# A local-attention stack on one core: squares summed as rows, norms spread by one-hot matmuls, q scaled right behind k, two passes reordered

## The reference

```python
q, k, v = split(x @ Wqkv)                      # 16 heads of width 64
q = l2norm(q) * q_scale;  k = l2norm(k) * k_scale
q = q*cos*scale + rotate_half(q)*sin*scale     # k with 1/scale
out = local_attention(q, k, v)                 # windows of 32, each looks at itself and the one before
x = x + out @ Wo
x = x + (a * gelu(gate)) @ W2                  # a, gate = split(layernorm(x) @ W1 + b1)
```

## Time and profile before

| | before |
|---|---|
| median of 3 runs | 4742.06 us (4739.58 to 4746.09) |
| the profiled execution, its own time | 4749.81 us |
| its span in the profile | 4748.0 us |
| busy PE / DVE / ACT / POOL | 93% / 74% / 52% / 52% |
| pass a0, first slots to the stack | about 0 to 580 us |
| stack (48 bodies) | about 580 to 4060 us |
| rotated pass and gated mix | about 4060 to 4748 us |

### The profile page before, as it was taken

One profiled execution on the slowest core, in us unless ns is written; L12 is line 12 of the kernel. 1 busy time (PEld: TensorE's weight loads), 2 busy tenths in 40 slices (PEclk: granted clock), 3 DMA queues, 4 the chain that ended last, 5 costly groups with the idle time before them and its releaser, 6 DMA issues. The chain is left out here.

```text
span 4748.0 us, 116556 instructions
## 1 busy us (share of the span) xinstructions
PE 4426.3 (93%) x46020; PEld 2614.7 (55%) x46020; DVE 3530.1 (74%) x3768; ACT 2451.6 (52%) x3764; POOL 2477.3 (52%) x3513
## 2 busy tenths in 40 slices
PE   7999889999999999999999999999999998678898
PEld 3333366666666666666666666666666665322233
DVE  5777478777778778778778778778778776477774
ACT  1666545554555555555455555545555554135564
POOL 1111266666666666666566666666666665122213
PEclk6999989999999999999999999999999999779999
DMA  3222122222222222222222223222222222222220
GB/s 88 56 55 55 55 51 63 57 58 71 63 61 61 55 74 72 53 61 61 73 65 59 57 60 81 57 62 57 57 72 58 58 61 71 42 55 46 48 45 19
DMA packets 182135, 281.98 MB, mean 59 GB/s; under 512 B 58269, under 2 KB 80349, under 8 KB 175965
## 3 DMA queue, kind: packets, MB, share of 16 engines
q1 hardware_dynamic: 154300, 241.72, 21.4%
q10 hardware_dynamic: 27648, 37.79, 3.5%
HBM read 61.77 MB, written 17.56 MB: 17 GB/s over the span
## 5 line engine op out<-in xcount | busy, mean ns | idle before, releaser
L1144 DVE SCALAR_TENSOR_TENSOR x<-l_r,l_qkvec,l_tab 128x1024 f32<-128x1024 f32 x768 | 936.3, 1278 | 31.0 <-ACT l_sq L1047 27.9
L553 DVE TENSOR_REDUCE a_nmax<-a_pair 128x2 f32<-128x1024 f32 x512 | 609.4, 1220 | 223.4 <-PE a_pair L676 223.3
L453 ACT ACTIVATE a_pt<-a_st 128x512 f32<-128x512 f32 x1024 | 543.2, 603 | 281.6 <-PE a_st L660 276.3
L974 POOL TENSOR_TENSOR l_ntmp<-l_seed 128x32 f32<-128x32 f32 (+1 forms) x480 | 112.1, 234 | 777.9 <-ACT l_seed L1030 759.1
L1001 POOL TENSOR_TENSOR l_u<-x 128x512 f32<-128x512 f32 x384 | 491.4, 1280 | 0.0
L1002 POOL TENSOR_TENSOR l_u<-x 128x512 f32<-128x512 f32 x384 | 490.2, 1276 | 0.0
L1317 PE MATMUL l_r<-xs,l_wqkv 128*128 (+1 forms) x768 | 424.6, 660 | 38.8 <-DVEq L1224 38.8
L1406 PE MATMUL l_r<-l_pbd,l_va 128*64 128x160 f32 (+1 forms) x6144 | 441.2, 296 | 18.8 <-DMA l_pbd<-l_pt 18.7
L1007 POOL TENSOR_TENSOR l_p<-l_p,l_srec 128x1024 f32<-128x1024 f32 x192 | 365.4, 1903 | 175.3 <-DVE l_srec L1236 142.0
L1406 PEld LDWEIGHTS l_r<-l_pbd,l_va 128*64 128x64 f32 x6144 | 395.3, 137 | 80.1 <-issue 80.0
L1367 PE MATMUL l_r<-l_kbd,l_qn 64*32 64x128 f32 x24576 | 418.5, 279 | 12.2 <-DMA l_kbd<-l_kn 6.6
(11 more groups left out here) (204 smaller groups left out, 7452.7 us busy)
## 6 DMA issues: line engine op xcount, KB each, us to landing
l_kbd<-l_kn SPq DMA_DIRECT2D x1536, 64.0 KB, 2.0
l_pbd<-l_pt SPq DMA_DIRECT2D x768, 64.0 KB
l_pbd<-l_pt ACTq DMA_DIRECT2D x576, 64.0 KB
a_ks<-a_scr SPq DMA_DIRECT2D x96, 192.0 KB
a_qs<-a_scr SPq DMA_DIRECT2D x288, 64.0 KB
a_scr<-a_parts SPq DMA_DIRECT2D x48, 256.0 KB, 2.5
l_pbd<-l_pt SPq DMA_DIRECT2D x192, 56.0 KB
l_wqkv<-in_wqkv SPq DMA_DIRECT2D x6, 1536.0 KB, 6.5
```

Source lines behind the costliest of these rows:

```text
L453: nc.scalar.activation(pt[n % 2][:, r, :], st[(4 * n + r + par) % 3][:], ACT.Exp, scale=SC).then_inc(exp_done, 1)
L553: nc.vector.tensor_reduce(out=nmax[:, n, 2 * i:2 * i + 2], in_=pair[i][:], op=ALU.max, axis=AX.X, negate=True).then_inc(pair_dve[i], 1)
L1144: last = nc.vector.scalar_tensor_tensor(out=t[a][:, 2 * half:2 * half + 2, :], in0=R[a][:, half, :].unsqueeze(1).to_broadcast([D, 2, T]), ...
```

## The change

In the stack:

- The squares of k are no longer added on POOL: TensorE adds the halves itself. The sums are made with the new matrix `block8` (8 columns) as the stationary side and the squares as the moving side, four groups of 128 tokens in four column tiles of the array, so that a head's sums stand as a row of 128 tokens. The norms become a 128x128 tile instead of 128x32, and so do the seed, the Newton steps, the reading on DVE and the zeros that clear R[3].
- ACT's expansion and the eight transposes go; `spread8`, a one-hot matrix of 64 rows to 128 columns, spreads the rows with eight matmuls, with a wait of PE for itself between the fourth and the fifth.
- q is scaled right behind k, ahead of the row sum.
- In the first three steps DVE turns P between the rotations of q and k. In the fourth step the sums of squares move up to the start, q is rotated before the residual is added, and v is projected between the mean and the variance.

In the rotated pass `QK_STEP` goes from 4 to 2, `ROWS_STEP` from 8 to 10, the splits from slots 6, 7, 7, 8, 9 to 5, 6, 7, 8, 9, and SP reads the row maxima behind the heads as in pass a0.

```diff
-        QK_STEP, ROWS_STEP = (4, 9) if rope is None else (4, 8)
+        QK_STEP, ROWS_STEP = (4, 9) if rope is None else (2, 10)
...
-                if m is not None and rope is not None:
-                    load_rows(0, par)
                 if s is not None:
...
-                if m is not None and rope is None:
+                if m is not None:
                     load_rows(0, par)
...
-                split_slots = (4, 5, 6, 7, 8) if rope is None else (6, 7, 7, 8, 9)
+                split_slots = (4, 5, 6, 7, 8) if rope is None else (5, 6, 7, 8, 9)
...
-        NSS = NT * 2 * CH
-        rnx = sb("rnx", [D, NSS, HALF])
+        NSS = D
+        spread8 = sb("spread8", [D, 2, 2, D])
...
-                        nc.gpsimd.tensor_tensor(sqs[0][:], sq[0][:, 0, :], sq[0][:, 1, :], ALU.add)
-                        nc.gpsimd.tensor_tensor(sqs[1][:], sq[1][:, 0, :], sq[1][:, 1, :], ALU.add).then_inc(S["sq_sum"], 1)
+                        nc.gpsimd.tensor_tensor(sqs[:], sq[0][:, 0, :], sq[0][:, 1, :], ALU.add).then_inc(S["sq_sum"], 1)
...
 ACT
-                    if has_ss and c < 3:
+                    if has_ss:
                         seeds(0, NSS, S["norm_ready"], S["seed_ready"])
...
+                        act.drain().then_inc(S["sq_ready"], 1)
...
-                        act.drain().then_inc(S["sq_ready"], 1)
+                        act.drain().then_inc(S["sqk_ready"], 1)
...
-                    if has_ss and c == 3:
-                        seeds(0, NSS, S["norm_ready"], S["seed_ready"])
...
-                    if has_ss:
-                        expand()
...
 DVE
-                    transpose_p(c)
+                    if c == 3 or b is None:
+                        transpose_p(c)
+                    if has_ss and c == 3:
+                        read_norm()
+                    if c == 3 and b is not None:
+                        rotate(0)
...
+                        nc.vector.engine_nop().then_inc(S["centred_pe"], 1)
...
-                    if c == 3 and has_ss:
-                        read_norm()
...
                     if b is not None:
-                        rotate(0)
+                        if c < 3:
+                            rotate(0)
+                            transpose_p(c)
                         rotate(1)
...
                         scale_by_norm(1)
-                        if c == 3:
-                            scale_by_norm(0)
+                        scale_by_norm(0)
...
-                    if has_ss and c < 3:
-                        scale_by_norm(0)
...
 PE
                         claim(3)
+                        pe.wait_ge(S["sqk_ready"], seen.next(S["sqk_ready"]))
+                        for half in range(2):
+                            for k in range(NT):
+                                nc.tensor.matmul(R[3][32 * k:32 * k + 2 * CH, 0, 0:D], block8[:, 1, :], sq[1][:, half, 128 * k:128 * k + 128],
+                                                 start=False, stop=False, skip_group_check=True)
                         pe.wait_ge(S["sq_sum"], seen.next(S["sq_sum"]))
                         for k in range(NT):
-                            for a in range(2):
-                                o = (k * 2 + a) * CH
-                                last = nc.tensor.matmul(R[3][:, 0, o:o + CH], sqs[a][:, 128 * k:128 * k + 128], block4[:],
-                                                        start=False, stop=True, skip_group_check=True)
+                            last = nc.tensor.matmul(R[3][32 * k:32 * k + 2 * CH, 0, 0:D], block8[:, 0, :], sqs[:, 128 * k:128 * k + 128],
+                                                    start=False, stop=True, skip_group_check=True)
...
-                    if has_ss and c < 3:
+                    if has_ss:
                         sums_of_squares()
...
-                    if c == 3 and has_ss:
-                        sums_of_squares()
...
+                    if has_var:
+                        pe.wait_ge(S["centred_pe"], seen.next(S["centred_pe"]))
+                    if b is not None:
+                        project_v()
+                    if has_var:
...
-                        pe.wait_ge(S["rnx_ready"], seen.next(S["rnx_ready"]))
+                        pe.wait_ge(S["rn_ready"], seen.next(S["rn_ready"]))
                         claim(0, "r0_dve_b", "r0_dve_b")
-                        for a in (1, 0):
-                            for k in range(NT):
-                                o = (k * 2 + a) * CH
-                                last = nc.tensor.transpose(R[0][:, 1 - a, 128 * k:128 * k + 128],
-                                                           rnx[:, o:o + CH, :].rearrange("p h i -> p (h i)"), C["ident"][:])
+                        for turn in range(2):
+                            for k in range(2):
+                                for half in range(2):
+                                    rows, a, o = slice(64 * half, 64 * half + 64), (half + turn + 1) % 2, 256 * half + 128 * k
+                                    last = nc.tensor.matmul(R[0][:, 1 - a, o:o + 128], spread8[rows, a, k, :], rn[rows, 0:D], start=True, stop=True)
+                                    if turn == 0:
+                                        last.then_inc(S["b_turn"], 1)
+                            if turn == 0:
+                                pe.wait_ge(S["b_turn"], seen.next(S["b_turn"], 4))
```

57 lines of the change are left out of this document (29 added, 28 removed).

## The result

| | before | after |
|---|---|---|
| median | 4743.43 us (4739.58 to 4746.09, 4 runs) | 4972.14 us (4960.14 to 4985.12, 4 runs) |
| ratio, 95% interval | 1 | 1.0483 [1.0455, 1.0512] |
| span of the profiled execution | 4748.0 us | 4983.3 us |

The change makes the kernel 4.8% slower: +229 us, where the forecast had +46 and its range ended at 4855 us. The direction was right, the size was not.

A forecast was written before the change was run, and what follows sets the result against it. It took DVE to bound a body's first steps and a chain through PE and DVE the rest; stack +89, clock -19, rotated pass -26, constant +2 gave +46 us, 4788 us against the median, range 4725 to 4855 us.

The forecast's parts named there:

- H: DVE, from reading the norms to rotating q: wait for q's square, now uncovered, plus wider norms; 1.29 us.
- the fifth boundary: PE, five tiling-mode changes a step instead of four: at most 19 us by the rows, possibly a whole drain each.
- The fourth step's chain: Stack's fourth step, third step's maximum until the scores begin: 21.19 us, with PE standing still for reading, seed and mask.
- the extra constant: Start of the stack: the additional constant adds some 2 us.
- a quarter back: Stack: low clock costs 74 us; sums go but new standstills come, so a quarter is regained, -19 us.
- the second loop: First steps: P's copies, product with v, new sums, q's projection and square, two rotations, P again; 13.1 us.
- DVE's at the 13.43 of the forecast: First steps, bounded by DVE: 13.43 us against 13.32, the removed POOL wait replaced by one as long.
- PE's wait for itself: Spread of the norms on PE: between nothing and 0.6 us, taken as 0.2.
- a clean body: One body of the stack without low clock: 1.89 us longer, 71.7 us; +89 us over 47 bodies.
- The clock was one: Rival, chance 0.18, faster: denser records keep the clock high in stack and rotated pass, giving 4707 us.
- The other three: Rivals: in between (0.10, no change, 4733 to 4750); tiles don't overlap (0.05, 5070); POOL becomes the bound (0.05, 4940).
- the tiles that don't overlap: Rival, chance 0.05, slower: sums on PE take 3.05 us, +8 us a body, 5070 us.

The follow-up runs named there:

- the new arithmetic alone: Changed kernel with DVE and ACT orders as before; sums as rows, k's halves on PE, spread by matmuls and the rotated pass's edits stay: 4824.13 us, ratio 1.0156.
- products in all three gaps: Changed kernel plus one unused product ahead of P by V in the first two steps, two ahead of the fourth step's scores: 4850.58 us, ratio 1.0208.
- The two fastest kernels: Rotated pass's edits; fourth step sums, last Wo products, q, mean, k; norms read behind P's turn: 4703.73 us (new sums and spread), 4703.26 us (old).

## Why the prediction was wrong in size

**What held.** Slower. H: in DVE's timeline of one body of after, 1.25 us lie between reading the norms and rotating q, where the forecast had 1.29:

```profile
1350.24 0.23 DVE L1166 TENSOR_SCALAR l_norm<-l_r 128x128 f32<-128x128 f32 x1
1351.49 2.48 DVE L1133 SCALAR_TENSOR_TENSOR x<-l_r,l_qkvec,l_tab 128x1024 f32<-128x1024 f32 x2 [1.02 <-ACT l_sq L1045]
```

POOL isn't the bound: its 128-column operations take 0.40, 0.46, 0.30 and 0.46 us, and the new arithmetic alone leaves the first two steps at 13.3 and 13.5. The sums overlap in their column tiles: 24 records from 1366.18 to the next start at 1366.95, 0.77 us, the forecast's 0.8, and this holds the change of tile shape to the projection behind them, so the fifth boundary has no cost that shows:

```profile
1366.18 0.62 PE L1296 MATMUL l_r<-l_sq,l_block 128*8 128x128 f32 x16
1366.95 1.98 PE L1313 MATMUL l_r<-xs,l_wqkv 128*128 x4
```

The fourth step's chain came out nearly term by term. In the body whose scores were shown above it takes 21.68 us from the third step's maximum (1283.39) to the scores (1305.07), against 21.19. The residual to the centring takes 1299.93 - 1297.15 = 2.78 us (forecast 2.79), PE waits 1.59 us for the mask; only H is longer there, 1294.75 - 1292.96 = 1.79 us instead of 1.29, because q's projection comes late on PE:

```profile
1292.96 0.29 DVE L1166 TENSOR_SCALAR l_norm<-l_r 128x128 f32<-128x128 f32 x1
1294.75 2.48 DVE L1133 SCALAR_TENSOR_TENSOR x<-l_r,l_qkvec,l_tab 128x1024 f32<-128x1024 f32 x2 [1.50 <-ACT l_sq L1045]
1297.15 0.68 DVE L1179 TENSOR_TENSOR xs<-xs,l_r 64x512 f32 x1
...
1299.93 0.69 DVE L1184 TENSOR_TENSOR l_xcn<-xs,l_r 128x512 f32<-128x512 f32 x1 [1.38 <-PE l_r L1330]
```

The rotated pass gives 19 us where the forecast had 26. The 2 us for the extra constant were not tested.

**The clock had the wrong sign.** The forecast took -19 us, "a quarter back", since the sums went. It named the new standstills in the same place and gave them no price. What it was can be read from the bodies whose mean granted clock is 1.00. In before they are 14 of 46, with a median of 69.80 us; in the changed kernel with products in all three gaps 35 of 46, with a median of 72.66. The mean bodies are 71.43 and, of after, 76.74, so the low level cost 1.6 us a body in before and costs 4.1 in after. This term was about +115 instead of -19: 134 of the missing 183 us. The experiment agrees: in that run the changed kernel needs 122 us less, though part of this is low clock that before has too. The term has two places. In the first two steps the products with v ran at the low level in many bodies, means of 3.0 and 2.8 us instead of 2.29; in the fourth the scores had a mean of 3.04 us instead of 2.36 (the spans of these groups, each step by itself). For the first two steps "it is idle time of an engine that no longer bounds this step" is the sentence that failed: the wait was free, what it did to the speed of the next product was not, and that product is in the loop. In the fourth step the forecast had the wait in its chain and the scores behind it at their old length, 24.22 us less the terms it named; that was wrong in the same way.

The Trainium skill's page "TensorE: Matmul & The Clock Gate", Part 4, has transposes not counted as PE activity as matmuls are; by it the change should have helped the clock. The two fastest kernels have the same order, one with transposes and one with matmuls (and with the old and the new sums), and mean clocks of 0.961 and 0.968 at the same time: the rule's sign may be right, but nothing came of it here.

**A loop without slack.** The forecast had the second loop at 13.1 us. The same sum by the rows of the run with P turned between the rotations, with the new sums, is 4.21 + 2.10 + 2.22 + 0.77 + 1.91 + 2.40 = 13.6 (in after itself the medians of the first two are 4.19 and 2.09); the term that was mis-sized is the way to the fifth copy, 4.21 + 2.10 instead of 3.81 + 2.0. So it was this loop, not DVE's at the 13.43 of the forecast, that bound, and the second step's median is 13.59. A loop that is itself the bound has nothing that could take up a slow product: every one at the low level went straight into the step.

**The third step is PE's.** I read it as part of one chain of DVE from the third maximum to the next body's, because the averages of the earlier trace rows don't separate steps. The step of before has no PE idle at all, and that of after, in windows, nearly none:

```profile
1605.90:1623.40 17.50, 17.50 (x201) 10.60 (x200) 12.96 (x12) 7.87 (x11) 10.86 (x14) 1.00 0.35 84
```

```profile
1351.38:1370.51 19.13, 19.04 (x234) 11.47 (x233) 15.30 (x15) 7.65 (x12) 14.52 (x21) 1.00 0.33 82
```

The first window is of before, the second of after. The sums now lie in this step (0.77), the spread takes 1.46 from its start to the next instead of 0.93, the scores 2.26 instead of 2.08, the rest 0.1: +1.6. No row showed the forecast's 0.2 for PE's wait for itself in the spread; measured, the spread is 0.4 to 0.5 above its 1.02, inside the bounds. Third and fourth step together are +1.94 a body where no scores are slow (19.09 + 26.31 in the run with products in all three gaps, 17.55 + 25.91 with the rotated pass alone) against a forecast of +1.67. The first two give 0.5 (twice 13.59 against twice 13.32) to 0.9 (13.79 + 13.49 with the added products against 13.06 + 13.31), where the forecast had 0.22. So a clean body is some 2.4 to 2.9 us longer instead of 1.89, the upper end by the bodies at full clock: 25 to 46 us of the miss.

Together 134 for the clock, 46 for the clean body and 7 for the rotated pass: 187 of 183. Where the clean body is taken shorter, the clock's part is larger by as much.

**The rivals.** The clock was one, but only in the direction that makes the kernel faster; the one with its sign turned wasn't among them. The other three didn't happen. Two of their numbers don't add up as written: the tiles that don't overlap were to cost 8 us a body and were summed with 6 (5070 us; with 8 it is 5164), and the chances of the list give 0.18 for faster and 0.72 for slower where the total says 0.20 and 0.70. Neither bears on the forecast. The range took in no case in which a standstill slows what comes behind it, so it ended 117 us too low.

## What to carry to other kernels

When an edit moves a producer behind another instruction, follow the data all the way round: P behind q's rotation put q's projection, square and rotation into a loop of copies, product and sums, made it the longest one, and on the old arithmetic this one move cost 4.6% (ratio 1.043 against 0.997). When it leaves PE standing still for a microsecond or two, price the product that comes next at the low clock too, and ask whether that product lies in a loop without slack; a throwaway product in the gap is a cheap test of it. An order that leaves no gaps was worth more here (24 us, 0.5%, beside the rotated pass) than arithmetic that saves PE time where it then stands (nothing).

## What the runs showed of the hardware that I had not expected

- Standing still for one to three microseconds cost PE its full clock for the work behind, in part of the cases: 2.24 us of idle time were followed by a product at 0.57 for 4.0 us, 2.70 us by 7.4 us at 0.54. Of the 92 products with v in the first two steps of 46 bodies of after, 37 took 3.5 to 4.3 us, behind waits of 1.44 to 3.56 us. It isn't the length alone: 28 others behind waits in the same range took 2.29 us, one of them behind 2.95 us, at full clock.

```profile
1256.07 2.29 PE L1411 MATMUL l_r<-l_pbd,l_va 128*64 128x160 f32 x32 [2.95 <-DMA l_pbd<-l_pt]
```

  What decides it wasn't settled by these runs.
- Useless work made the kernel faster: one product of 0.95 us in each of two steps of a body gave 97 us, nearly half of them in another step.
- The scores take 2.03 us in some steps and 2.1 to 2.3 in others at a granted clock of 1.00, in before too (2.15 in the third step). Why isn't known.
- q scaled right behind k costs only 33 us, though P's chain gets 1.2 us longer in each step; the first step gained 0.7 us and the other three lost 1.4 in all, and which waits took it up was not looked into.
